# Output projection of attention with seven block products (Strassen-Winograd) in place of eight, sums read off one accumulating PSUM bank

## What is computed

```python
def _L0_attn_ref(q, w_qkv, w_dense):
    ...                                   # NHEADS, KVHEADS, HEAD_D = 32, 8, 128
    qkv = q @ w_qkv.T
    ...
    probs = jax.nn.softmax(scores, axis=-1)      # causal
    attn = jnp.einsum('bkgst,btkd->bskgd', probs, vh)
    attn = attn.reshape(Bq, Sq, NHEADS * HEAD_D)
    return attn @ w_dense.T               # the output projection, 4096 -> 512
...
x = x + 0.5 * _L0_ffn_ref(_layernorm(x, axis=-1), ...)
x = x + _L0_attn_ref(_layernorm(x, axis=-1), L0_attn_w_qkv, L0_attn_w_dense)
x = x + 0.5 * _L0_ffn_ref(_layernorm(x, axis=-1), ...)
```

## Time and profile before

| | |
|---|---|
| median of 3 runs | 1143.31 us (1141.67 to 1143.67) |
| the profiled execution: own time | 1153.05 us |
| its span, first to last instruction | 1151.2 us |
| mean granted TensorE clock | 0.989 |
| attention, first slot to the start of L1241 | 212.2 to 960.8 us of the span |
| TensorE matmuls busy | 1107.8 us, 96% of the span |
| VectorE, ScalarE, GpSimd busy | 671.1, 569.2, 466.9 us |

### The profile page before, as it was taken

One profiled execution on the slowest core, in us unless ns is written; L12 is line 12 of the kernel. 1 busy time (PEld: TensorE's weight loads), 2 busy tenths in 40 slices (PEclk: granted clock), 3 DMA queues, 4 the chain that ended last, 5 costly groups with the idle time before them and its releaser, 6 DMA issues.

```text
span 1151.2 us, 19600 instructions
## 1 busy us (share of the span) xinstructions
PE 1107.8 (96%) x6008; PEld 928.5 (81%) x6008; DVE 671.1 (58%) x1809; ACT 569.2 (49%) x1513; POOL 466.9 (41%) x484
## 2 busy tenths in 40 slices
PE   8889998899999999999999999999999999889996
PEld 6667877788888888888888888888888887667875
DVE  7668868754454545454545445454544557568866
ACT  4257753474455536446444545553553543257740
POOL 1546647154235325315323432522531420546643
PEclk9989999999999999999999999999999999999998
DMA  9995565001101100101010010110100006935555
GB/s 356 411 331 193 186 231 187 20 1 38 56 1 38 55 0 36 55 0 36 0 55 0 36 55 0 36 55 0 36 0 1 1 17 276 375 101 176 185 168 187
DMA packets 38617, 114.80 MB, mean 100 GB/s; under 512 B 4384, under 2 KB 4384, under 8 KB 36512
## 3 DMA queue, kind: packets, MB, share of 16 engines
q1 hardware_dynamic: 33440, 97.30, 23.3%
q0 software_dynamic: 5120, 16.78, 4.3%
HBM read 79.20 MB, written 34.87 MB: 99 GB/s over the span
## 4 chain that ended last, share of the span: by engine, by line
PE 83%; DVE 6%; ACT 3%; another core or an unknown queue 3%; issue 2%; DMA 2%; POOL 1%; SPq 0%; DVEq 0%; ACTq 0%; POOLq 0%
PE bank L1373 22%; PE bank L1405 15%; PE bank L1474 9%; PE bank L1434 9%; PE bank L1348 6%; PE bank L1386 6%; PE bank L1359 4%; PE bank L1262 4%; PE bank L1309 2%; DMA xn<-x_rows 1%; PE bank L1470 1%; PE bank L1430 1%; PE bank L1241 1%; PE bank L1281 1%
## 5 line engine op out<-in xcount | busy, mean ns | idle before, releaser
L537 POOL TENSOR_TENSOR scores<-scores,pinv 128x512 f32<-128x512 f32 (+3 forms) x256 | 176.7, 722 | 353.2 <-DVE pinv L1085 353.2
L480 POOL TENSOR_TENSOR tback_lo<-experts,tback_hi 128x768 fp32r<-128x768 f32 x62 | 114.3, 1846 | 83.2 <-ACT tback_hi L643 83.2
L705 ACT ACTIVATE pT_hi<-bank 128x512 fp32r<-128x512 f32 (+2 forms) x192 | 87.0, 488 | 112.4 <-PE bank L1386 112.4
L734 ACT ACTIVATE scores<-scores,nmax 128x512 f32<-128x512 f32 (+3 forms) x256 | 140.3, 558 | 0.0
L750 ACT ACTIVATE oT_hi<-bank 128x512 fp32r<-128x512 f32 x64 | 38.3, 599 | 204.3 <-PE bank L1470 204.3
L1059 DVE TENSOR_TENSOR pT_lo<-bank,pT_hi 128x512 fp32r<-128x512 f32 (+2 forms) x192 | 101.0, 554 | 52.7 <-ACT pT_hi L705 52.7
L1077 DVE CUSTOM_DVE_ANT_0 scores<-bank,causal 128x512 f32<-128x512 f32 (+3 forms) x256 | 112.3, 487 | 1.3 <-issue 0.3
L1063 DVE TENSOR_TENSOR oT_lo<-bank,oT_hi 128x512 fp32r<-128x512 f32 x64 | 44.3, 692 | 106.9 <-ACT oT_hi L750 106.9
L1373 PE MATMUL bank<-xnT_hi,wqs_hi 128*128 128x512 f32 x256 | 106.3, 415 | 0.0
L1405 PE MATMUL bank<-wds_hi,oT_hi 128*128 128x512 f32 x256 | 106.0, 414 | 0.0
L1373 PE MATMUL bank<-xnT_lo,wqs_hi 128*128 128x512 f32 x256 | 100.8, 394 | 0.0
(11 more groups left out here) (207 smaller groups left out, 2881.0 us busy)
## 6 DMA issues: line engine op xcount, KB each, us to landing
experts<-in_ffn_w SPq DMA_DIRECT2D x32, 768.0 KB
xn<-x_rows SPq DMA_DIRECT2D x62, 256.0 KB, 2.8
y_rows<-xn SPq DMA_DIRECT2D x62, 256.0 KB, 2.0
raw_q<-in_wq SPq DMA_DIRECT2D x8, 1024.0 KB
raw_d<-in_wd SPq DMA_DIRECT2D x8, 1024.0 KB
x_rows<-experts SPq DMA_DIRECT2D x1, 7936.0 KB, 30.0
raw_w<-in_ffn_w SPq DMA_DIRECT2D x8, 768.0 KB, 5.2
raw_kv<-in_wkv SPq DMA_DIRECT2D x8, 512.0 KB, 3.3
```

The lines of the kernel that those rows point to most:

```text
L480: nc.gpsimd.tensor_tensor(tback[par][1][:], experts[:, bass.ds(at + FRONT, GU - FRONT)], tback[par][0][:].bitcast(F32), ALU.subtract).then ...
L537: nc.gpsimd.tensor_tensor(s, s, pinv[k % 2][:, i:i + 1].to_broadcast([P, P * (i + 1)]), ALU.mult).then_inc(att.normed, 1)
L705: nc.scalar.activation(pT[0][:, lo_col:hi_col], bank[b][:, 0:hi_col - lo_col], ACT.Copy).then_inc(att.t_hi, 1)
L734: nc.scalar.activation(s, s, ACT.Exp, bias=nmax[par][:, i:i + 1], scale=-1.0, accum_out=psumr[par][:, i:i + 1]).then_inc(att.exp, 1)
```

## The change

The 512 tokens x 4 heads of a quad are taken as a 2x2 block matrix: rows are token halves (first and last 256), columns are the even and odd heads of the two head pairs. The weights of a group are a 2x2 block matrix too: rows even and odd heads, columns the two halves of the 512 outputs. Seven products of sums of such blocks take the place of eight products of blocks. Each product is 12 matmuls of 128x256: 2 token tiles, 2 head pairs, 3 parts.

- **PE**: `dense` does one product. Slots with r = 1, 2, 3 do two products, the first between steps 2 and 3 above, the second where `dense` was; slots with r = 0 do one, where it was. Within a quad a11, s2, s3, a22 add up in bank 2, then a12 starts it anew, then s1 starts it anew and s4 adds to it. After each product DVE adds the bank to its quarter of x (`add_product`), and the next product waits for that (`att.added`).
- **The left operands**: after a pair's first head ACT copies the whole head to `first_o` and makes the high part of a11; after the second head it makes the high parts of a12, a22, s3, s1, s2, and in the next slot s4. DVE makes the sums (`left_sum`, four for a pair) and the seven low parts of 128x256.
- **The right operands**: seven high parts on ACT and seven low parts and four sums on POOL for a group, in place of four and four, now in slots k = 2 to 6. The sums are made in place in `raw_d`, each from the one before.
- **PE waits** before each product for the low parts of both operands; the wait for `att.pv_lo` before step 6 is now one for the last copy of bank 1 (`evacuated`).
- **The end**: slot 63 does a12 and s1, slot 64 s4 and the last quad's a11, slot 65 the other six products in the order `LAST`; slots 66 to 68 are gone. DVE's `statistics` for the next layer stand in slot 64 ahead of the low parts of unit 63. SP's loads of the next layer's experts wait for the last product.

Semaphores that only the first feed-forward layer uses are made once; that adds and removes no instruction.

```diff
+PRODUCTS = ("a11", "s2", "s3", "a22", "a12", "s1", "s4")
+WEIGHT = {"a11": "b11", "s2": "t2", "s3": "t3", "a22": "t4", "a12": "b21", "s1": "t1", "s4": "b22"}
+FRESH = ("a11", "a12", "s1")
+LAST = ("a11", "a12", "s2", "s1", "s3", "s4", "a22")
...
+            def rights(g, k):                                  # POOL
+                def low(i):
+                    n = RIGHT.index(i)
+                    pool.wait_ge(att.right_hi, NP * g + n + 1)
...
+                def combined(i, a, b):
+                    nc.gpsimd.tensor_tensor(raw_b[i], raw_b[a], raw_b[b], ALU.subtract).then_inc(att.right_sum, 1)
+                if k == 2:
+                    low("b11")
+                    combined("t1", "b12", "b11")
+                    combined("t3", "b22", "b12")
+                if k == 3:
+                    low("t3")
+                if k == 4:
+                    low("t1")
+                    combined("t2", "b22", "t1")
+                    low("t2")
+                if k == 5:
+                    combined("t4", "b21", "t2")
+                    low("t4")
+                if k == 6:
+                    low("b21")
+                    low("b22")
...
-                    if k == 4:                                 # ACT
+                    for i in {2: ("b11",), 3: ("t3",), 4: ("t1", "t2"), 5: ("t4",), 6: ("b21", "b22")}.get(k, ()):
+                        right_hi(g, i)
+                    cuts(g, k, high_part)
...
+                def heads(g, k):                               # ACT
+                    u = 8 * g + k
+                    act.wait_ge(att.pv_mm, u)
+                    if k % 2:
+                        wait(act, att.left_lo, NP * (4 * g + k // 2))
+                        nc.scalar.activation(first_o[:], bank[1][:], ACT.Copy)
+                        left_hi(g, k, "a11", bank[1][:, 0:2 * P])
+                    else:
+                        left_hi(g, k, "a12", bank[1][:, 0:2 * P])
+                        left_hi(g, k, "a22", bank[1][:, 2 * P:])
+                        left_hi(g, k, "s3", o_diff[:])
+                        left_hi(g, k, "s1", first_o[:, 2 * P:])
+                        left_hi(g, k, "s2", first_o[:, 0:2 * P])
...
+                    late = r in (1, 3) and exists(u, 3, UNITS + 1)   # DVE, in slot
+                    if isinstance(u, int) and u == UNITS:
+                        add_product(products(g, k)[-1], b=0)
+                        norm_then = statistics(2, 0)
+                    if late:
+                        for i, src in (("s3", o_diff[:]), ("s1", first_o[:, 2 * P:]), ("s2", first_o[:, 0:2 * P])):
+                            left_lo(g, k - 1, i, src)
+                        left_sum(first_o[:, 0:2 * P], bank[1][:, 0:2 * P], first_o[:, 0:2 * P], ALU.subtract)
                     if exists(u, 1, UNITS):
                         turned_lo(u - 1, 0, COL[0], COL[1], 6)
                         turned_lo(u - 1, 1, COL[1], COL[2], 7)
...
+                    if r and todo and exists(u, 0, UNITS):
+                        add_product(todo.pop(0), b=(k - 5) // 4 % 2)
...
-                def dense(g, u, k):                            # PE
+                def dense(product, g, k):
+                    i, before, o_bank = product
...
+                    pe.wait_ge(att.left_lo, 2 * NP * quad + NP + LEFT.index(i) + 1)
...
+                    for half in range(2):
                         m = 0
-                        for h in range(G):
+                        for head_pair in range(2):
                             for a, z in PARTS:
-                                last = nc.tensor.matmul(o_bank(u)[:], oT[ob][h][a][:, tile * P:(tile + 1) * P],
-                                                        wds[h][z][:], start=(m == 0), stop=(m == 3 * G - 1))
+                                last = nc.tensor.matmul(o_bank[:, half * 2 * P:(half + 1) * 2 * P],
+                                                        left(i, head_pair, b)[a][:, half * P:(half + 1) * P],
+                                                        right[WEIGHT[i]][z][:, head_pair], start=(fresh and half + m == 0),
+                                                        stop=(half == 1 and m == 5), skip_group_check=True)
```

More of the change, by code:

```diff
@@ L155, in build @@
             wvs = pair("wvs", [P, HC, D], st)
-            wds = [pair(f"wds{r}", [P, HID], st) for r in range(G)]
+            right = {i: pair(f"right_{i}", [P, 2, HID // 2], st) for i in ("b11", "t2", "t3", "t1")}
             kT = [pair("kT0", [P, SEQ], st), None]
@@ L160, in build, with left_block @@
             kT[1] = pair("kT1", [P, SEQ], st)
-            oT[0][G - 1] = pair(f"oT0_{G - 1}", [P, SEQ], st)
-            oT[0][:G - 1] = [pair(f"oT0_{r}", [P, SEQ], st) for r in range(G - 1)]
+            left0 = [{}, {}]
+            def left_block(i, parities):
+                block = pair(f"left0_{i}_{len(parities)}{parities[0]}", [P, 2 * P], st)
+                for b in parities:
+                    left0[b][i] = block
+            for i in ("a22", "s3"):
+                left_block(i, (0, 1))
+            for i in ("a12", "s1", "s4"):
+                left_block(i, (0,))
+            for i in ("a11", "s2"):
+                left_block(i, (0, 1))
+            left_block("a12", (1,))
             vT = sb("vT", [P, SEQ], F32, st)
@@ L265, in att_tail, with products, quad_of, left @@
                 slot(KV - 1, k)
-        def o_bank(u):
-            return bank[(0, 1, 2, 3)[u - UNITS - 1] if isinstance(u, int) and u > UNITS else 2]
         UNITS = KV * BATCH * G
+        def products(g, k):
+            u = 8 * g + k
+            if isinstance(u, int) and u > UNITS:
+                done = NP * (2 * KV - 1)
+                if u == UNITS + 1:
+                    return [(i, done + LAST.index(i), bank[LAST_BANK[i]]) for i in LAST]
+                return []
+            if not exists(u, 5, UNITS):
+                return []
+            first = 2 * ((k - 5) % 4)
+            done = 2 * NP * (g + k // 8) + DONE[k % 8]
+            return [(i, done + n, bank[0 if isinstance(u, int) and u >= UNITS - 1 and i in ("s1", "s4") else 2])
+                    for n, i in enumerate(PRODUCTS[first:first + 2])]
+        def quad_of(g, k):
+            return 2 * g + (k - 5) // 4
+        def left(i, head_pair, b):
+            return left1[i] if head_pair else left0[b][i]
+        def last_read(i, g, k, head_pair):
+            quad = 2 * g + (k - 1) // 4
+            b = (k - 1) // 4 % 2
+            back = 1 if head_pair or left0[0][i] is left0[1][i] else 2
+            return NP * (quad - back) + PRODUCTS.index(i) + 1
+        def evacuated(g, k):
+            quad, r = 2 * g + k // 4, k % 4
+            if r == 0:
+                return att.left_lo, 2 * NP * (quad - 1) + NP + 1
+            if r == 1:
+                return att.left_sum, 2 * len(SUMS) * quad
+            if r == 2:
+                return att.left_lo, 2 * NP * quad + 1
+            return att.left_sum, 2 * len(SUMS) * quad + len(SUMS)
         PROJ_AHEAD = 4
@@ L292, in cuts @@
             flat = "p c d -> p (c d)"
[L293 to L297 removed]
+            base = 6 + 6 * g
             if exists(8 * g + k, 0, UNITS - 9):
@@ L1063, in low, with add_product @@
                     nc.vector.tensor_tensor(dst, src, hi.bitcast(F32), ALU.subtract).then_inc(s, 1)
+                def add_product(product, b):
+                    i, before, o_bank = product
+                    half, c = BLOCK[i]
+                    part = x[:, 4 * b + 2 * half:4 * b + 2 * half + 2, c * (HID // 2):(c + 1) * (HID // 2)]
+                    dve.wait_ge(att.o_mm, before + 1)
+                    if isinstance(before, int) and before >= NP * (2 * KV - 1):
+                        for p in [p for p in LAST[:LAST.index(i)] if BLOCK[p] == BLOCK[i]][-1:]:
+                            dve.wait_ge(att.added, NP * (2 * KV - 1) + LAST.index(p) + 1)
+                    nc.vector.tensor_tensor(part, o_bank[:].rearrange("p (t c) -> p t c", t=2), part,
+                                            ALU.add).then_inc(att.added, 1)
@@ L1096, in slot @@
                         low(qT[1][:, P:], bank[0][:, P:], qT[0][:, P:], att.proj_out)
-                    if exists(u, 5, UNITS + 4):
-                        tile = (3, 4, 5, 6, 7, 0, 1, 2)[k % 8]
-                        dve.wait_ge(att.o_mm, u - 4)
-                        nc.vector.tensor_tensor(x[:, tile, :], o_bank(u)[:], x[:, tile, :], ALU.add).then_inc(att.added, 1)
+                    if late and exists(u, 0, UNITS):
+                        left_lo(g, k - 1, "s4", first_o[:, 0:2 * P])
+                    for product in todo:
+                        add_product(product, b=(k - 5) // 4 % 2)
                     if exists(u, 1, UNITS):
-                        ru, bu = (k - 1) % 4, ((k - 1) // 4) % 2
-                        dve.wait_ge(att.pv_hi, u)
-                        low(oT[bu][ru][1][:], bank[1][:], oT[bu][ru][0][:], att.pv_lo)
+                        heads(g, k)
```

(3 more changed lines are left out.)

200 lines of the change are left out of this document (143 added, 57 removed).

## The result

| | before | after |
|---|---|---|
| median, us | 1143.49 (4 runs, 1141.67 to 1145.42) | 1160.03 (4 runs, 1159.77 to 1164.26) |
| profiled execution, us | 1153.05 | 1159.88 |
| its span, us | 1151.2 | 1158.1 |
| attention, first score matmul of slot 1 to the first gate-up matmul, us | 741.48 | 758.34 |

The ratio is 1.0152, with a 95% interval of 1.0131 to 1.0174: the changed kernel is 16.5 us slower. The two profiled executions differ by only 6.8 us, because that of before lay 9.6 us above its median; the difference arose outside attention. Inside (slot 0, 7.0 us in both, is left out), the traces differ by 16.86 us (219.27 to 960.75 against 218.51 to 976.85), as much as the medians differ by.

A forecast was written before the change was run, and what follows sets the result against it. PE, busy 100.00 of every 100 us in attention, was taken as the bound; -16.1 (PE's saving) + 23.7 (lateness in groups) + 5.2 (end of attention) = +12.8 us, giving a median of 1156.1 us, range 1137 to 1164.

The forecast's parts named there:

- The signs on record: Expected trace marks: PE idle about 2.5 us in slot 5, ACT idle about 2.6 before t2's copy, low parts above 425 ns.
- PE's saving, -16.1 us: Output projection: seven half-width products for eight, 161.3 us of matmuls in place of 177.4, by distances of 0.120 and 0.231.
- The seam rival: Every product has a seam at its start, 0.1 us each for 112 products, +11 us, 1167 us; chance 0.10.
- Slot 5, 2.5 us: Each group's slot 5: pT_hi late behind ACT's wait for POOL's t2, 2.2 us, plus 0.3 from DVE and POOL meeting.
- they meet t1's low part and hold up t2's sum: +0.3 us: Slot 5: DVE operations with two SBUF inputs meet POOL's low part of t1 and delay its sum t2, 0.3 us.
- the detour stays hidden: Slot 5: ACT's copies and POOL's two operations end before PE needs pT_lo; -6.5 us, 1136.8 us; chance 0.20.
- that left 2 us: Slot 5 before the change: ACT was late by 3.4 us without harm, and PE had 2 us to spare.
- Slots 1, 3 and 7, 0.6 us a group: DVE's added operations, in slots 3 and 7 meeting POOL's, make additions or products late, 0.2 us in each slot.
- The tail, 5.2 us: End of attention, slots 63 to 65: PE waits for low parts, statistics and the last head's pieces, +5.2 us, bounds 3 to 7.
- the 0.7 of the forecast: Slot 63 has no projection, so its second transposes come at 5.5 and wait 0.7 us for pT_lo.
- ports collide each time: Slots 3 and 7: each meeting of DVE and POOL costs a whole POOL operation, +3 us, 1159 us; chance 0.05.

The follow-up runs named there:

- e5: e2 with pT_lo and the product's addition put ahead of the low parts of s3 and s1 on DVE; 1134.76 us, ratio 0.9935.
- e3: The changed kernel with ACT's copy of t2 reading b22 and not waiting for POOL's sum (a wrong t2); 1163.11 us, ratio 1.0183.
- e7: The kernel before with four more 128x512 copies on ACT ahead of pT_hi in slot 5 of each group; 1156.23 us, ratio 1.0122.
- e2: e1 with POOL's sum t4 and low part of b21 also moved out of slot 5, to slots 3 and 6; 1144.95 us, ratio 1.0017.
- e1: The changed kernel with POOL's weight sums in another order and earlier, so ACT never waits for one in slot 5; 1147.91 us, ratio 1.0050.
- e6: The changed kernel with only DVE's order altered: pT_lo and the product's addition ahead of the low parts of s3 and s1; 1158.98 us, ratio 1.0162.

## Why the prediction was right or wrong

The direction was right, and 1160.0 lies in the range of 1137 to 1164. The signs on record came too: PE idle in slot 5 (1.92 us in two stops, forecast 2.5), ACT idle before the copy of t2 (2.92, forecast 2.6), low parts with SBUF inputs at 738 ns on average against 419 with one in PSUM. Of +12.8 us against +16.5, the terms:

- **PE's saving, -16.1 us: right.** Where nothing is late (e5) a group is exactly 2.0 us shorter. The distances were the right ones; by the rule of the Trainium skill, "TensorE: Matmul & The Clock Gate", section "Back-to-back issue gap", the -19.4 would have been 91.6 us a group, 0.4 below the measured. The seam rival (a tenth of a microsecond for each product) is excluded by the same 91.99.
- **Slot 5, 2.5 us: size right, reason half right.** The product came at 9.51 us against the forecast 9.3, and ACT's copies, POOL's sum and `pT_hi` (7.09 against 6.82) came in the forecast order. The step "they meet t1's low part and hold up t2's sum: +0.3 us" holds as far as it goes: the sum took 1.48 us, against 1.29 where DVE is out of the way. What failed is that it ends there. DVE's operations stretch much more than POOL's (the second of them took 1.51 us against 0.42), and three in a row made DVE ready for `pT_lo` only at 7.0, about as late as ACT. My rival "the detour stays hidden" looked only at the ACT and POOL side, and would have failed for the same reason: e3 hides the detour and gains nothing. Its "that left 2 us" was misread as well: the 2.07 us are from the start of `pT_hi` to the transposes, and `pT_lo` stands between them; it started at 633.98 and took 0.69, so 0.8 was left. In e7 a `pT_hi` 2.1 us later cost 1.4.
- **Slots 1, 3 and 7, 0.6 us a group: too much.** They cost 0.1 together in the changed kernel (slot 3 is the one to watch: POOL's fourth operation made it lose 1.06 in e2). With them a group should have taken 95.1; the short kind took 94.5.
- **The clock: missing.** Four of the six full groups lost another 1.5 us, and the last head 1.2: some 7 us. I had said nowhere what the stall would do to TensorE's level. This and the overestimate of slots 1, 3 and 7 (0.5 x 8 = 4 us) cancel in part, which is luck: the total looks better than its parts.
- **The tail, 5.2 us: too low by the part not seen.** 2.4 us in slot 64 came as 2.37, 1.9 behind the last head as 1.58. Missing was slot 63: without a projection in front of it the slot is shorter, and POOL's low part of b21, which normally hides behind one, ends 1.6 us too late. e1, which makes b21 earlier, shows no such wait, but one of 0.74 for `pT_lo`, the 0.7 of the forecast, which the longer one had covered.

In sum: -16.1, slots 5 with the small ones some 20 (8 x 2.5), the clock 7, the tail 6: 16.9 us, the difference of the traces.

The rival **ports collide each time** had the right mechanism and looked for it in slots 3 and 7, where nothing came of it, instead of in DVE's share of slot 5. The exclusive lock of the Trainium skill, "SBUF — State Buffer", section "SBUF: two separate sides", agrees with e2 and e3, where DVE's two operations end 0.28 and 0.27 us after POOL's two. It speaks of whole operations, and should have been followed through DVE's queue as well as POOL's.

## What to carry to other kernels

A releaser names the wait that ended last. Before taking it away, follow every other engine that feeds the same instruction to the moment when it would have been ready; if that is about as late, nothing is won until both are moved, and an experiment that removes one alone can read as "not the cause" (e3, e6). Count for each time slot what POOL has to do, and keep DVE's operations with two SBUF inputs behind whatever TensorE waits for: they are not slow, but beside a POOL operation they end when it does. And where an engine is at 100%, saved instructions are worth their full time only as long as nothing becomes late: 30 us lie here between two kernels that issue the same numbers of matmuls, copies and sums in another order.
